# Six local-attention layers: the product Wv Wo made once a layer, probabilities applied to the shifted inputs, work moved between the vector, scalar and pool engines, and new orders on every engine

## The reference

```python
def shift_tokens(t):                       # second half of the features from the token before
    a, s = jnp.split(t, 2, -1)
    s = jnp.pad(s, ((0, 0), (1, 0), (0, 0)))[:, :-1]
    return jnp.concatenate([a, s], -1)
...
q = l2norm(q) * qs                         # 16 heads of 64
k = l2norm(k) * ksc
q = q * cos * scale + rotate_half(q) * sin * scale
k = k * cos * inv + rotate_half(k) * sin * inv
out = local_attention(q, k, v)             # 32 queries see their own window of 32 keys and the one before
return out @ Wo
...
for i in range(DEPTH):
    x = attn_layer(shift_tokens(x), Wqkv[i], q_scale[i], k_scale[i], Wo[i]) + x
    x = ffn_layer(shift_tokens(x), ln_g[i], ln_b[i], W1[i], b1[i], W2[i], b2[i]) + x
```

## Time and profile before

| | us |
|---|---|
| median of three executions | 2145.36 (2140.11 to 2148.38) |
| profiled execution, span from first to last instruction | 2143.9 |
| first layer, up to the first instruction of the six layers on PE | about 459 |
| one tile in the middle of the span (82 tiles between 600 and 2000 us) | 17.1 |

### The profile page before, as it was taken

The page is one execution under the profiler, slowest core; times in us unless marked ns, Lnnn a source line. Parts: engine busy times, 40 slices in busy tenths (PEclk is TensorE's granted clock), DMA queues, the critical chain, the costliest instruction groups (busy, mean ns, idle before and its releaser), DMA issues.

```text
span 2143.9 us, 84229 instructions
## 1 busy us (share of the span) xinstructions
PE 2022.6 (94%) x35763; PEld 1356.1 (63%) x35763; DVE 1497.0 (70%) x2268; ACT 1286.6 (60%) x1844; POOL 1522.5 (71%) x2307
## 2 busy tenths in 40 slices
PE   4789999878999999999999999999999999999997
PEld 1455555545666667666766667666676666766675
DVE  2445454458877887777877787777877788778773
ACT  3567777634656665665656565566656666566653
POOL 3344444458878887788877778778887788777880
PEclk8899999998999999999999999999999999999998
DMA  4999999932323222242222422224222242222221
GB/s 125 289 347 355 344 357 344 348 126 61 74 62 111 68 65 65 63 113 67 72 62 62 113 62 69 65 62 120 63 66 62 63 117 70 62 62 63 68 72 43
DMA packets 120004, 261.51 MB, mean 122 GB/s; under 512 B 29092, under 2 KB 34128, under 8 KB 118864
## 3 DMA queue, kind: packets, MB, share of 16 engines
q1 hardware_dynamic: 119632, 256.13, 41.4%
HBM read 87.06 MB, written 68.29 MB: 72 GB/s over the span
## 4 chain that ended last, share of the span: by engine, by line
PE 68%; POOL 4%; DVE 3%; issue 2%; ACT 1%; POOLq 0%; DVEq 0%; ACTq 0%
PE ring L463 22%; PE ring L529 9%; PE ring L473 8%; PE yps L541 7%; PE ring L499 7%; PE ring L569 5%; PE ring L510 4%; PE tpose L579 3%; PE ring L491 1%; POOL roped L275 1%; DVE turned L643 1%; PE tpose L551 1%; DVE ss L652 1%; DVE stats L701 0%; POOL ss L248 0%
## 5 line engine op out<-in xcount | busy, mean ns | idle before, releaser
L643 DVE TENSOR_TENSOR turned<-ring,ropes 128x1024 f32<-128x1024 f32 x384 | 452.0, 1219 | 303.0 <-PE ring L463 303.0
L240 POOL TENSOR_TENSOR roped<-turned 128x512 f32<-128x512 f32 x384 | 522.5, 1386 | 170.4 <-PE ring L473 169.0
L463 PE MATMUL ring<-wqkv,xT 128*128 128x512 f32 x1152 | 567.4, 616 | 5.2 <-ACT xT L328 4.0
L275 POOL TENSOR_TENSOR roped<-roped,rnorm 128x1024 f32<-128x1024 f32 x192 | 361.5, 1904 | 7.5
L1170 POOL TENSOR_SCALAR less<-less,lowest 128x512 f32<-128x512 f32 x256 | 175.3, 697 | 240.0 <-DVE lowest L1139 240.0
L1139 DVE CUSTOM_DVE_ANT_0 less<-ps_b,shifted 128x512 f32<-128x512 f32 x256 | 166.6, 688 | 226.0 <-PE ps_b L1002 79.7
L463 PEld LDWEIGHTS ring<-wqkv,xT 128*128 128x128 f32 x1152 | 198.2, 192 | 161.0 <-issue 149.8
L369 ACT COPY pT<-ring 128x1024 f32<-128x1024 f32 x96 | 97.2, 1012 | 305.8 <-PE ring L510 305.8
L529 PEld LDWEIGHTS ring<-pT,vwin 64*64 64x64 f32 x12288 | 198.5, 134 | 51.9 <-issue 51.5
L317 ACT ACTIVATE squares<-ring 128x1024 f32<-128x1024 f32 x192 | 197.3, 1028 | 55.8 <-DVE turned L643 55.8
L529 PE MATMUL ring<-pT,vwin 64*64 64x32 f32 x12288 | 219.7, 220 | 4.9 <-issue 3.4
(11 more groups left out here) (133 smaller groups left out, 3234.7 us busy)
## 6 DMA issues: line engine op xcount, KB each, us to landing
vwin<-v SPq DMA_DIRECT2D x1536, 64.0 KB, 2.0
shifted<-scratch_w SPq DMA_DIRECT2D x64, 1024.0 KB, 12.6
scratch_w<-wrows SPq DMA_DIRECT2D x48, 1026.0 KB, 10.9
scratch_w<-x SPq DMA_DIRECT2D x16, 1026.0 KB, 10.4
wqkv<-in_l_wqkv SPq DMA_DIRECT2D x6, 1536.0 KB, 6.9
wo<-in_l_wo SPq DMA_DIRECT2D x6, 512.0 KB
w<-in_l_w SPq DMA_DIRECT2D x6, 342.0 KB
w<-in_l_w SPq DMA_DIRECT2D x6, 171.0 KB
```

Of the source, the lines that this page charges most:

```text
L240: nc.gpsimd.tensor_tensor(halves[2][:, :, side, :], halves[0][:, :, side, :], halves[1][:, :, 1 - side, :], ALU.add).then_inc(s[name + "_a ...
L275: nc.gpsimd.tensor_tensor(whole, whole, norm, ALU.mult).then_inc(s[name + "_roped"], 1)
L463: last = nc.tensor.matmul(out[:, half, :], xT[:, t % SEQT * P:(t % SEQT + 1) * P], wqkv[:, layer_of(t), at + half * 512:at + (half + 1) * ...
L643: ins = nc.vector.tensor_tensor(turned[:, n, part, :].rearrange("p (h d) -> p h d", d=DH), heads, table, ALU.mult)
```

## The change

1. Values. v is no longer projected. Once a layer PE turns Wv (`turn_wv`, eight transposes) and multiplies it by Wo head by head (`make_wvo`, 16 matmuls), with ACT copies. `attend` multiplies the probabilities by the shifted input itself, of which SP keeps two copies per tile in `xs` (the tile's own rows and the rows one window earlier), in eight matmuls of 32 rows by 128 by 512 columns. Its result is twice as large, so `copy_o` is two copies of 128x1024, and `project_out` takes 16 matmuls, in two halves a period apart.
2. Probabilities. They are divided on POOL and transposed in blocks of 32x32 by DVE straight to SBUF (`turn_p` on DVE); PE's transposes and ACT's copy go.
3. Masks. ACT copies the mask into PSUM (`write_masks`); PE's eight matmuls go.
4. q's sums. One of the two halves of `add` for q is done by DVE (`join_q`). `roped` has two buffers.
5. Norms. The root takes 11 small POOL instructions after the clamp where it took 13.
6. FFN shift. Two transfers an SP group (`shift` on SP) write `behind`; PE's matmuls go.
7. Orders, PSUM rooms and the buffer of xT's transposes are new.

The core of the diff:

```diff
+            def windows(t):
+                half, here, before = D // 2, t % TILES, (t - 1) % TILES
+                a, b = t % NX, (t - 1) % NX
...
+                at_least(sp, s["o_summed"], t - NX + 1)
...
+                sp.dma_start(xs[:, a, 0, 0:half], x[:, here, 0:half]).then_inc(s["own_in"], 16)
+                sp.dma_start(xs[1:P, a, 0, half:D], x[0:P - 1, here, half:D]).then_inc(s["own_in"], 16)
...
+                sp.wait_ge(s["own_in"], OWN * (t + 1))
+                sp.dma_start(xs[W:P, a, 1, :], xs[0:P - W, a, 0, :]).then_inc(prev_in[a], 16)
+                sp.dma_start(xs[0:W, a, 1, :], xs[P - W:P, b, 0, :]).then_inc(prev_in[a], 16)
+            def shift(g):
+                sp.wait_ge(s["y_added"], SEQT * (g + 1))
...
+                sp.dma_start(behind[1:P, :, :], x[0:P - 1, at:at + SEQT, half:D]).then_inc(s["behind_in"], 16)
+            def divide(t):
+                if live(t):
+                    pool.wait_ge(s["rinv_made"], t + 1)
+                    whole = probs[:, t % 2, :, :]
+                    nc.gpsimd.tensor_tensor(whole, whole, rinv[:, :].unsqueeze(2).broadcast_to([P, HEADS, W2]), ALU.mult
+                                            ).then_inc(s["p_normed"], 1)
+            def write_masks(t):
...
+                    rows = bias[:, 1 if t % SEQT == 0 else 0, :, :].unsqueeze(1).broadcast_to([P, 2, PAIRS, W2])
+                    nc.scalar.copy(ring[:, room("S"), :, :].rearrange("p r (j k) -> p r j k", k=W2), rows).then_inc(s["masked"], 1)
+            def attend(t):
+                    pe.wait_ge(s["p_turned"], t + 1)
...
+                    for own in (1, 0):
+                        for win in range(WT):
+                            rows = slice(W * win, W * win + W)
+                            last = nc.tensor.matmul(outs[win // 2][:, win % 2, :], xs[rows, t % NX, 1 - own, :],
+                                                    pT[rows, own, :, :].rearrange("p h q -> p (h q)"),
+                                                    start=own == 1, stop=own == 0, skip_group_check=True)
+            def join_q(t):
+                if live(t):
+                    dve.wait_ge(s["q_rotated"], t + 1)
+                    at_least(dve, s["q_turned"], t - 1)
+                    join_halves(nc.vector, 0, t, DVE_HALVES, s["q_joined"])
+            def turn_p(t):
+                if live(t):
+                    dve.wait_ge(s["p_normed"], t + 1)
+                    at_least(dve, s["o_summed"], t)
+                    nc.vector.transpose(pT[:, :, :, :], probs[:, t % 2, :, :].rearrange("p h (o k) -> p o h k", k=W)
+                                        ).then_inc(s["p_turned"], 1)
```

More of the change, by code:

```diff
@@ L146, in halves_of @@
             half = D // 2
-            return x[:, g % BATCH * SEQT + tile, 0:half], bank("XS")[:, tile * half:(tile + 1) * half]
+            return x[:, g % BATCH * SEQT + tile, 0:half], behind[:, tile, :]
         def live(t):
@@ new lines, in turn_wv, with make_wvo @@
+            def turn_wv(layer):
+                if layer is not None:
+                    pe.wait_ge(s["weights"], LOADS * (layer + 1))
+                    out = take("T", layer).rearrange("p b c -> p (b c)")
+                    for j in range(PAIRS):
+                        last = nc.tensor.transpose(out[:, j * P:(j + 1) * P], wv[:, j * P:(j + 1) * P], ident[:, :])
+                    last.then_inc(s["wv_turned"], 1)
+            def make_wvo(layer):
+                if layer is not None:
+                    pe.wait_ge(s["wvT_copied"], layer + 1)
+                    for half in range(2):
+                        out = take("M", layer, half)
+                        for j in range(half * PAIRS // 2, (half + 1) * PAIRS // 2):
+                            for r in range(2):
+                                rows, at = slice(r * DH, (r + 1) * DH), j % (PAIRS // 2) * D
+                                last = nc.tensor.matmul(out[:, r, at:at + D], wvT[rows, j, :], wo[rows, j, :], start=True, stop=True)
+                        last.then_inc(s["wvo_made"], 1)
@@ L495, in scores @@
+            def scores(t):
+                if live(t):
+                    pe.wait_ge(s["qT_copied"], t + 1)
+                    pe.wait_ge(s["kT_copied"], t + 1)
+                    pe.wait_ge(s["masked"], t + 1)
+                    out = take("S", t)
+                    for j in range(PAIRS):
                         for win in range(WT):
@@ L535, in project_out @@
-            def project_out(t):
-                if live(t):
-                    pe.wait_ge(s["oT_copied"], t + 1)
-                    pe.wait_ge(s["weights"], LOADS * (t // (SEQT * BATCH) + 1))
-                    out = take("Y", t)
-                    for j in range(PAIRS):
-                        last = nc.tensor.matmul(out[:, 0:D], oT[:, j % 2, j // 2, :], wo[:, layer_of(t), j, :], start=j == 0,
-                                                stop=j == PAIRS - 1)
-                    last.then_inc(s["y_made"], 1)
@@ L545, in shift @@
[L545 to L554 removed]
+                    last.then_inc(s["scored"], 1)
@@ new lines, in project_out @@
+            def project_out(t, half):
+                if live(t):
+                    if half == 0:
+                        pe.wait_ge(s["oa_copied"], t + 1)
+                        pe.wait_ge(s["ob_copied"], t + 1)
+                        pe.wait_ge(s["wvo_copied"], 2 * (t // (SEQT * BATCH) + 1))
+                        take("Y", t)
+                    out = view("Y")
+                    for h in range(half * PAIRS, (half + 1) * PAIRS):
+                        r, j = h // PAIRS, h % PAIRS
+                        last = nc.tensor.matmul(out[:, 0:D], oT[:, h, :], wvo[:, layer_of(t), r, j, :],
+                                                start=h == 0, stop=h == HEADS - 1)
+                    if half == 1:
+                        last.then_inc(s["y_made"], 1)
```

441 lines of the change are left out of this document (213 added, 228 removed).

## The result

The changed kernel takes 2216.64 us in the median (2211.06 to 2221.25, four runs) against 2144.83 us before. The ratio is 1.033, 95% interval 1.0295 to 1.0365: slower by 3.3%, where 2070 was forecast. The profiled execution has a span of 2214.5 us.

A forecast was written before the change was run, and what follows sets the result against it. PE was taken as full before; after, PE 15.15, POOL 14.6, DVE 14.1 us a tile, so order decides. At 16.15 a tile instead of 17.07: 2143.9 - 83 + 8 = 2069, median 2070 us; range 2015 to 2160.

The forecast's parts named there:

- step 3: Period of four with the FFN statistics: 15.6 us, including 1.51 of statistics and 0.6 for the shift's late landing.
- The layout: Hand-laid order of four periods, 14.0 + 14.0 + 17.9 + 15.6 = 61.5 us, 15.4 a tile; chance 0.53, range 2040 to 2105.
- ordinary periods: Periods without much FFN work, taking the longer of two loops: 14.0 us each.
- POOL's loop: Loop two, from k's sum of squares through root, scalings, division, transposition and two sums: 14.0 us.
- Wv Wo: Making the product once a layer, eight transposes and 16 matmuls on PE: 4.4 us, taken as 0.25 a tile.
- The 0.5 a tile for what such a sum missed: Allowance added to the period sum, after the 0.49 us a tile that PE's pieces had left unexplained before.
- loop one: From end of scores to end of next scores, through DVE's 9.59 us and PE's values and scores: 13.5 us.
- step 1: Period of four with 5.15 us of FFN matmuls on PE: 17.9 us, with PE leading.
- The port: Shared by DVE and POOL: `join_q` behind a POOL scaling would wait up to 1.9 us; argued clear of POOL's adds.
- The rivals: PE alone paces (0.16, 2024); POOL and its port (0.14, 2142); dear transposition (0.10, 2151); values not overlapping (0.07, 2490).

The follow-up runs named there:

- The cut: The changed kernel with its 127-row transfer into `behind` split into 112 and 15 rows; 2052.47 us, 0.9518 of before.
- the one with three tiles early: The changed kernel with the small first-row transfer and three of four tiles of the 127-row transfer issued one period earlier; 2033.53 us, 0.9503 of before.
- the early issue: The changed kernel with the 112 and 15 row split, plus the small first-row transfer into `behind` issued one period earlier; 2042.83 us, 0.9465 of before.

## Why the prediction was wrong

- **The step that failed** is the last term of step 3: "against two issues and 2.0 to landing; I allow 0.6". It measures 7.16 (171.9 / 24). The 2.0 was the landing of a 32-row `vwin` transfer, taken for one of 127 rows by four tiles. From the end of `add_y` to the statistics it took 10.4 us, where the work of DVE between them covered 2.9 (1206.83 to 1209.77). The row's form did not match in the number of pieces, 508 here, nor in the rate: about one DMA engine's share is busy. The cut, the kernel without transfers and the one with three tiles early each take the wait away, all but 0.9 us a group of it or less, and the time with it.
- **What a gap that long does beside itself** was not in the sum: PE idles 5.9 us, falls to the lower clock level (0.56 granted in the rows above) and loses about 1 us more a group. This is read from the rows; the difference of 20.6 us agrees.
- **The layout held.** Without the wait the same kernel takes 0.9518 of before, where 2070 / 2145 is 0.965: in most groups its periods are 13.4, 15.2 to 16.1, 13.4 and 17.9 against the layout's 14.0, 15.6, 14.0 and 17.9. It was 0.6 high in the ordinary periods: POOL's loop, 14.0 by the sum, takes no more than 13.4. Over 90 periods the pitch is 15.65 us against 16.15. Wv Wo was priced too low: the two periods of a layer in which it is made take 18.8 and 18.5 us (from 941.42 and 960.17), some 8 us over the usual, where the sum had 4.4. The 0.5 a tile for what such a sum missed happened to cover it.
- **Ranking of the engines.** That PE's total work doesn't pace the ordinary periods is shown by the kernel with half of the output matmuls: PE has more time and the periods stay. That POOL doesn't either is read from the waits: 79 transpositions wait 7.0 us in all for POOL, while DVE waits 1.3 us a tile for the scores and the values wait for the transposition, which is loop one. That PE alone leads in step 1 is refuted by the same kernel.
- **The port.** `join_q` lies clear of POOL's passes, as argued (692 ns in the mean). The price of the earlier trace rows comes back where the division is put back on DVE, with 1.94 us for 1.22.
- **The rivals.** None of the four was it. The range, 2015 to 2160, held only causes in compute; each transfer but one was waved through for its lead in periods, and the one without lead got the price of another shape.
- **The parts together.** The rest of the change is worth more than was forecast, and one transfer a group hid it: with that cut, the kernel is 5% faster than before. The fastest complete versions measured, 0.9436 and 0.9438, add the early issue and the cut of `xs`, and are not told apart from one another.

## What to carry to other kernels

Price a transfer by its own shape: the number of contiguous pieces, and how many DMA engines are busy with them. A shift by one partition makes 127 of 128 rows, which here kept 7.7% of 16 engines busy; as 112 and 15 rows the same work kept 33.1% busy and took about a quarter of the time. And when work is moved from an engine to a transfer, look at what lies between its last input and its first reader: here 2.9 us of cover stood against 10.4.

## What the hardware showed that was not expected

- About one DMA engine's share moved 64 pieces of 256 bytes a microsecond inside SBUF (319 in 5 us); while they are under way, the next transfer's issue on the same queue shows as 7.03 us, against 0.73 when it is issued a period earlier. A long issue row can be the symptom of the transfer ahead of it.
- The transposition of 128x1024 float32 in blocks on DVE costs 1.24 us, like any other pass, and eight matmuls of 32 rows by 512 columns, laid on four row groups, overlap: 16 records of 0.62 us, 2.02 us for all.
- The same division is 1.90 us on POOL, and on DVE 1.22 to 2.84 in one kernel (median 1.90). The one shown above of 2.82 began behind a scaling on POOL:

```profile
L741 DVE TENSOR_TENSOR probs<-probs,rinv x96: 1224/1900/2844, 515.4 to 2227.5; 128x1024 f32<-128x1024 f32 x96
```
